# Attention and mixture of experts in one kernel: where in a quad the value transposes, the expert counts and the transposition of x are queued

## What is computed

```python
q, k, v = split((x @ w_qkv + b_qkv).reshape(B, 16, S, 24), 3)     # B=8, S=512, x: (8, 512, 128)
vals = softmax(q @ k.T / sqrt(8)) @ v
x = layernorm(x + vals.transpose(0, 2, 1, 3).reshape(B, S, 128) @ w_out + b_out)
gates = sigmoid(x @ Wg)                        # 8 experts
w = top-2 gates, normalised, scattered to (T, 8)
out = (silu(x @ Ws1) * (x @ Ws3) @ Ws2  +  sum over e of w[:, e] * (silu(x @ We1[e]) * (x @ We3[e]) @ We2[e])) / 3
x = layernorm(x + out)
```

## The kernel before

| step | job | who reads it |
|---|---|---|
| 0 | proj (i = 2): output projection, L536 | DVE L607 |
| 1 | mT: transposition of the row maxima, L524 | DVE L599, L601, then a DMA to the key/query stack |
| 2 | counts (i = 1, from the second batch on): two matmuls that count rows per expert, L497, L498 | DVE L384, L387 |
| 3 | valsT: four transpositions of the value product of quad q - 2, L528, from pv_sb, which ACT copies at the start of the stage (L896) | DVE L587, L593 |
| 4 | xT: transposition of the next x tile, L506 | ACT L555 |
| 5 | x1T (i = 3): L541 | ACT L572 |
| 6 | qkv: projections of xT, L512, L513, L517 | ACT L562, L566 |
| 7 | oT (i = 1): L531; gate (i = 3): L547 | ACT L570; ACT L576 |

## Time and profile before

### The profile page before, as it was taken

How to read it: one execution, slowest core, us unless ns; L and a number is a source line. 1 busy time by engine, 2 the same in 40 slices (tenths; PEclk the granted TensorE clock), 3 DMA queues, 4 the chain that set the end, 5 groups by cost and what they waited for, 6 DMA issues and landing times.

```text
span 698.8 us, 16083 instructions
## 1 busy us (share of the span) xinstructions
PE 641.5 (92%) x4593; PEld 313.8 (45%) x4593; DVE 549.5 (79%) x1272; ACT 425.8 (61%) x973; POOL 270.1 (39%) x402
## 2 busy tenths in 40 slices
PE   1899999999899999999999999999899989999970
PEld 1232333343334343343433334323248878888760
DVE  4875777778787998999799799797658757878882
ACT  2055777777567667777676766776734246666652
POOL 3122232122325324423433532440515416677772
PEclk9999999999999999999999999999989999999995
DMA  4366556443414433333332443230132033454522
GB/s 78 58 127 177 127 118 152 106 95 89 83 44 80 101 75 68 90 62 87 80 79 53 84 101 70 65 88 12 52 106 58 27 81 88 121 160 134 155 83 75
DMA packets 161857, 62.68 MB, mean 90 GB/s; under 512 B 110586, under 2 KB 155516, under 8 KB 161808
## 3 DMA queue, kind: packets, MB, share of 16 engines
q1 hardware_dynamic: 155008, 46.72, 30.7%
q0 software_dynamic: 5648, 13.26, 6.2%
q10 hardware_dynamic: 1152, 2.10, 0.8%
HBM read 38.04 MB, written 24.26 MB: 89 GB/s over the span
## 4 chain that ended last, share of the span: by engine, by line
PE 61%; issue 10%; POOL 10%; DMA 6%; DVE 6%; ACT 4%; SPq 2%; POOLq 0%; ACTq 0%; DVEq 0%
PE pvp L1021 17%; PE scoreB L1001 16%; PE scoreA L987 15%; POOL y_dram L1212 6%; DMA parts_dram<-parts 3%; DVE mx L931 2%; ACT prob L904 2%; PE shared L528 2%; POOL slots_dram L491 2%; DMA ks<-parts_dram 2%; PE shared L517 2%; PE shared L536 1%; POOL prob L1197 1%; PE shared L512 1%; PE shared L547 1%
## 5 line engine op out<-in xcount | busy, mean ns | idle before, releaser
L931 DVE TENSOR_REDUCE mx<-scoreA 128x2 f32<-128x1024 f32 x256 | 305.6, 1219 | 73.7 <-PE scoreA L987 71.2
L904 ACT ACTIVATE prob<-scoreB 128x512 f32<-128x512 f32 x512 | 279.7, 600 | 122.4 <-PE scoreB L1001 122.0
L987 PE MATMUL scoreA<-ks,qs 72*128 72x512 bf16 x512 | 206.6, 411 | 15.9 <-DMA ks<-parts_dram 13.4
L1001 PE MATMUL scoreB<-qs,ks 74*128 74x512 bf16 x512 | 201.6, 396 | 6.3 <-ACT prob L904 3.0
L1021 PE MATMUL pvp<-prob,v 128*32 128x512 f32 x1024 | 139.9, 620 | 0.8 <-ACT pv_sb L896 0.8
L987 PEld LDWEIGHTS scoreA<-ks,qs 72*128 72x128 bf16 x512 | 51.2, 102 | 158.1 <-DVE mx L931 73.8
L1001 PEld LDWEIGHTS scoreB<-qs,ks 74*128 74x128 bf16 x512 | 50.0, 99 | 102.1 <-ACT prob L904 79.0
L1212 POOL DMA_INDIRECT y_dram<-prob x72 | 70.9, 985 | 44.9 <-issue 30.3
L831 POOL CAST parts<-qk 128x256 bf16<-128x256 f32 x32 | 12.7, 398 | 187.9 <-ACT v_raw L566 168.4
L491 POOL DMA_INDIRECT slots_dram<-rows,slot_i x64 | 63.4, 991 | 55.9 <-DMA ks<-parts_dram 30.8
L1571 PE MATMUL scoreB<-w,prob 128*128 x288 | 44.0, 276 | 0.9 <-DVE prob L1384 0.9
(11 more groups left out here) (174 smaller groups left out, 892.8 us busy)
## 6 DMA issues: line engine op xcount, KB each, us to landing
qs<-parts_dram SPq DMA_DIRECT2D x96, 96.0 KB
parts_dram<-parts SPq DMA_DIRECT2D x32, 192.0 KB
slots_dram<-blank POOLq DMA_DIRECT2D x9, 520.0 KB
prob<-slots_dram SPq DMA_DIRECT2D x72, 65.0 KB, 1.9
ks<-parts_dram SPq DMA_DIRECT2D x64, 64.0 KB
prob<-y_dram SPq DMA_DIRECT2D x8, 512.0 KB
ks<-parts_dram SPq DMA_DIRECT2D x32, 96.0 KB
xin<-in_L_attn_x SPq DMA_DIRECT2D x32, 64.0 KB, 2.2
```

Source lines behind the costliest of these rows:

```text
L904: act.activation(prob[:, i % 2, j, 2 * u + c, :], scoreB[:, c], ACT.Exp, scale=SCALE).then_inc(exp_done, 1)
L931: dve.tensor_reduce(mx[:, i % 2, at // 2, at % 2 * 2:at % 2 * 2 + 2], scoreA[:, at % 2], AX.X, ALU.max).then_inc(max_done, 1)
L987: ins = pe.matmul(scoreA[:, at % 2, c], qs[0:KR, st, j, qc * P:(qc + 1) * P], ks[0:KR, st, j, :], start=True, stop=True)
L1001: pe.matmul(scoreB[:, c], ks[0:KM, i, j, kc * P:(kc + 1) * P], qs[0:KM, i, j, :], start=True, stop=True).then_inc(b_ready, 1)
```

## The change

The table `Jobs.at` gets another order, and DVE's sequence follows. valsT goes from step 3 to step 2 in every stage. In a counting stage, counts goes from step 2 to step 4 and xT from step 4 to step 5; the copies of the counts go to step 4 on DVE, and `place` parts 0, 1, 2 go from steps 3, 5, 7 to steps 5, 6, 7. Beside the shared expert, valsT comes ahead of counts. The change adds a line at the top, so that line numbers from L83 on are higher by one after it.

```diff
--- before.py
+++ after.py
@@ -80,11 +80,12 @@
             kinds.append("x1T")
         if at == 1 and (inner or 0 <= s + 1 < self.quads):
             kinds.append("mT")
-        if at == 2 and i == 1 and (inner or 2 <= b <= self.batches):
+        counting = i == 1 and (inner or 2 <= b <= self.batches)
+        if at == 2 and (inner or 0 <= s - 2 < self.quads):
+            kinds.append("valsT")
+        if at == 4 and counting:
             kinds.append("counts")
-        if at == 3 and (inner or 0 <= s - 2 < self.quads):
-            kinds.append("valsT")
-        if at == 4 and (inner or s + 4 < self.quads):
+        if at == (5 if counting else 4) and (inner or s + 4 < self.quads):
             kinds.append("xT")
         if at == 7 and i == 3 and (inner or 1 <= b <= self.batches):
             kinds.append("gate")
@@ -943,10 +944,10 @@
                             dve.wait_ge(const_done, CONSTS)
                         choose(dve, b - 2, at - 1)
                         choose(dve, b - 2, at)
-                    if i == 1 and at == 2 and routing(b):
+                    if i == 1 and at == 4 and routing(b):
                         read_counts_job(dve, b)
-                    if i == 1 and at >= 3 and at % 2 and routing(b):
-                        place(dve, b - 2, at // 2 - 1)
+                    if i == 1 and at >= 5 and routing(b):
+                        place(dve, b - 2, at - 5)
                     if i == 2 and finishing(b):
                         statistics(dve, b, at)
                     if i == 2 and at >= 5 and at % 2 and routing(b):
@@ -1068,7 +1069,7 @@
         late_owner = shared[0:1, 0:P]
 
 
-        BESIDE = {0: ("counts", "valsT"), 1: ("oT",), 2: ("proj",), 7: ("x1T",), 8: ("gate",)}
+        BESIDE = {0: ("valsT", "counts"), 1: ("oT",), 2: ("proj",), 7: ("x1T",), 8: ("gate",)}
         COUNT_AT, OWNER_AT = 16, 24
         STAGE_OF = {"counts": 1, "valsT": 1, "oT": 1, "proj": 2, "x1T": 3, "gate": 3}
 
@@ -1250,8 +1251,8 @@
             def beside(n):
 
                 if n == 0:
+                    dve_job(dve, "valsT", B, 1)
                     read_counts_job(dve, B)
-                    dve_job(dve, "valsT", B, 1)
                 elif n in (1, 2):
                     place(dve, B - 2, n - 1)
                 elif n == 3:
```

## The result

The kernel after takes 686.17 us (median of six runs, 684.44 to 690.92), the kernel before in six runs beside it 695.8 (691.49 to 697.25): ratio 0.9892, 95% interval 0.9862 to 0.9923, so 7.5 us faster on 695.8, with an interval of 5.4 to 9.6. (The ratio on record is of the runs of both kernels and not of the two medians, which lie 9.6 apart.) The prediction said 686.5 from a base of 692.57. Its gain of 6.1 us lies inside the interval. That 686.17 comes within 0.3 us of 686.5 is luck: the base is 3.2 higher than the one it was worked out from. It gave 0.57 to a change within 1% and 0.38 to more; 1.1% was measured, and the interval, 0.8 to 1.4%, holds the 1%.

The account below looks back on a forecast made before the run. PE was taken to set the pace, losing 0.25 us to ACT in step 3 of stages that don't count. 4.75 + 0.1 + 0.3 + 0.9 = 6.05, say 6.1, off 692.57 gave 686.5 us; range 682.0 to 691.0.

Parts of the forecast that it names:

- The steady gain: Stages that don't count: valsT at step 2 fills PE's wait for ACT in step 3; 0.25 us each, 19 stages, 4.75.
- stage 28: Gains nothing, since PE idles 0.41 us in stage 29 for DVE's split maximum anyway.
- stage 29: No x to turn, so the last wait falls away and the longer wait in step 5 is filled; 0.3 us won.
- stages 30 and 31: The transpositions fit whole into PE's 0.47 us idle for ACT in step 3; 0.9 us won for the two.
- Stages 5 and 8: Their gain is not kept: they run into waits for the stack's keys, whose transfers were started too early to follow.
- DVE's cover in stage 16: DVE reads valsT between two maxima, the second still ready for A of step 5; fits by 0.16 us.
- The slower rival: Counting stages: DVE's count copies late as `place` crowds steps 4 to 7; 3.7 us slower, 696.3; chance 0.10.
- Counting stages: Stages 13, 17, 21, 25: gains and losses of steps 2 to 5 sum to 0.03 us each, 0.1 over four.
- Stages 8 to 10: Stages 8 and 9 run into the 2.17 us wait at stage 10, which stays, so their gain is lost.
- The end: What follows stages 30 and 31 starts earlier by as much; beside the shared expert valsT and counts swap for nothing.
- The clock in the tail: Rival: behind stage 31 denser stages 30 and 31 keep the clock up; 3.4 us more, 683.1; chance 0.13.
- The sum's last figure, 685.9: Forecast time if the waits of stages 6 and 10 don't bind in an unprofiled run, 0.25 x 2 more.

Follow-up runs that it names:

- e2: Kernel after, but counting stages and the step beside the shared expert keep the order before; 691.36 us, ratio to before 0.9941.
- e4: Kernel after, but in stages with i = 0 and 2 x's transposition goes to step 2 and valsT to step 4; 690.48 us, ratio to before 0.9952.
- e1: The kernel before, unchanged, run and profiled once more; 694.42 against 695.44 us, ratio 0.9992.
- e7: Kernel after, but in counting stages xT stays at step 4, counts goes to step 5, `place` moves later; 690.42 us, ratio to before 0.9926.
- e3: Kernel before with the new order in counting stages only, valsT at step 3 elsewhere; 694.47 us, ratio to before 0.9997.
- e11: Kernel before with 44 unused transpositions of the identity on PE ahead of its first scores; 693.89 us, ratio to before 0.9987.
- e5: The kernel after, unchanged, run and profiled a second time; 687.86 us, ratio to before 0.9883.
- e8: Kernel after with the edits of e6 and e7 together; 686.87 us, ratio to before 0.9863.
- e6: Kernel after, but the row maxima's transposition (mT) at step 0, not 1, in stages with i = 0, 1, 3; 684.62 us, ratio to before 0.984.
- e10: Kernel after with 18 unused transpositions of the identity on PE ahead of its first scores; 691.13 us, ratio to before 0.9925.

## Why the prediction was right, and where not

**The steady gain** came as worked out. ACT's wait of 0.25 in step 3 went whole, the transpositions cost 0.44 ahead of a score as they had behind one, and each stage lost 0.22 to 0.28. e2 and e4 show that it is the filled place that counts. Added up against e1: nineteen stages at 0.25, stage 28 0.26, stage 29 0.05, stages 30 and 31 0.88, in all 5.9 of the 6.1 us. Stages 5 and 8 gained nothing, as said. Stage 28 was put at nothing and stage 29 at 0.3; it came the other way round, with the same sum. Stage 29 still waits for DVE's split maximum, now with valsT behind it. Timeline of PE, kernel after, stage 29, step 2:

```profile
460.94 0.66 PE L529 MATMUL shared<-ident,pv_sb 128*128 128x128 f32 x4 [0.59 <-DVE m L602]
```

**DVE's cover in stage 16** was said to fit by 0.16 us. It does, to the hundredth. e2, e4 and e7 show how little stands behind it: in each DVE comes late in some stages, and PE pays 0.36 to 0.71 us there. The slower rival had named the wrong place, though. DVE was late not behind `place` in counting stages, but at the split maximum, for which PE's next job waits.

**Counting stages** came out at no change, as said, with two larger terms off that cancel: counts cost 0.36 between two scores, not 0.47, so PE comes 0.1 earlier to x's transposition and waits 0.34 there, not 0.24. DVE has the counts copied 1.55 behind the start of its maximum (291.55 to 293.10); 1.54 was predicted. The wait is DVE's time, so making PE faster ahead of it wins nothing.

**Stages 8 to 10** are the step that failed: "such transfers were started too early to follow". PE's wait for the keys at stage 10 fell from 2.17 to 0.90 and the clock stayed up behind it, about 2.8 us in the profiles of after and e3. No term of the sum had PE's code in it. These 2.8 us are shown for the profiled executions only. The times of e3 and e11, whose profiles have them too, show 0.2 and 0.9 us with intervals of about 2 to either side. In runs without a profile the code load may fall elsewhere, and stage 1 alone took from 15.48 to 18.34 us in the thirteen profiles, which can hide such a gain; that stays open.

**The end** was said to start earlier by as much as PE gains, and the changed order beside the shared expert to cost nothing. In after, e3, e5 and e8 the shared expert takes 1.6 to 1.9 us more than in e1. That the order isn't the cause is seen in e4, e6, e7 and e10, which have it and take 47.6; what after, e3, e5 and e8 have in common and no other profile has is that the scatter's last packets come late, at the end of a packet of queue 8. The sum had no term for this either.

**The clock in the tail** was a rival with a chance of 0.13, and in the profiles of after, e4 to e7 and e10 the half clock behind stage 31 is gone. But filling stages 30 and 31 doesn't settle it: e2 has them filled too, and there the half clock is as long as before (6.8 us); e8 has them filled and shows half of it, 3.4 us, and so does e3, which has them unfilled. It was argued against with the rule that a transposition doesn't count as PE being busy as a matmul does (the Trainium skill, "TensorE: Matmul & The Clock Gate", Part 4: PE-mode transpose); with e2 on one side and after on the other, no run here decides on that rule. What holds the clock there stays open.

If all of this were in every run, 5.9 + 2.8 + 2.7 - 1.6 would give 9.8 us: just outside the 5.4 to 9.6 of the first comparison and inside the 6.0 to 10.3 of e5. The steady 5.9 alone is inside the first and just outside the second. So the steady gain, which the prediction had worked out, is shown stage by stage; how much of the rest is in a typical run is not, and the closeness of the totals doesn't tell. (The sum's last figure, 685.9, should read 686.0.)

## What to carry to other kernels

On an engine that works in order, look for the distance between starts where it should be constant: a gap ahead of an instruction that waits for a slower engine is filled by any job that is due anyway, at no cost, as long as the reader of that job has room. Read that reader's slack first, here 0.16 us: where e2, e4 and e7 used it up, single stages lost more than the filled gap wins. An unexplained gain in the first round of a loop may come from the place of a code load there, and a few instructions more or less ahead of it show whether it is.

## What was not expected of the hardware

- With a 16 KB packet of queue 8, taken here for PE's code and 0.9 to 1.6 us long, beside a store of 192 KB, what waited for the store came 0.8 to 1.7 us later, and SP's two small transfers took 3.15 to 3.44 us to issue instead of 2.6. Beside the last scatter of the routed rows such a packet put off the landing: DVE waited 2.67 to 2.93 us for it in four profiles and 0.96 to 1.09 in the other nine.
- Small DVE instructions beside an elementwise POOL instruction ended with it, 0.39 to 0.60 us long instead of 0.15 to 0.18 (e2). This agrees with the Trainium skill ("SBUF — State Buffer", SBUF: two separate sides), by which a DVE operation with two inputs in SBUF and a GpSimd operation that reads SBUF hold a shared pair of ports for a whole instruction each and the other one waits.
- At stage 10 the granted clock was at its lower level, 1.2 GHz, in the five profiles in which PE had waited 1.62, 1.82, 1.97, 2.04 and 2.17 us for the keys. In the eight in which it had waited 0.37 to 1.40 it stayed at 2.4.
